# One scatter in place of two between attention and expert layers: residual rows carry their mean and reciprocal root, and sorted tiles are normalised behind their load

## What is computed

```python
x = x + attn(_layernorm(x), ...)          # linear attention: elu(q) (elu(k)^T silu(v)), head norm, gate, Wo
x = x + experts(_layernorm(x), itok, ctx) # 4 experts chosen by token number: silu(x G_e^T) * (x U_e^T), then D_e
x = x + ffn(_layernorm(x), W_up, W_gate, W_down)   # weights made ternary
```

## Time and profile before

| | us |
|---|---|
| median of 3 runs | 717.07 (715.48 to 717.67) |
| the profiled execution, its time | 716.13 |
| its span (first to last instruction) | 714.3 |
| TensorE busy | 686.1 |
| VectorE busy | 501.3 |
| ScalarE busy | 295.6 |
| GpSimd busy | 230.2 |

### The profile page before, as it was taken

The page is one execution under the profiler, slowest core; times in us unless marked ns, Lnnn a source line. Parts: engine busy times, 40 slices in busy tenths (PEclk is TensorE's granted clock), DMA queues, the critical chain, the costliest instruction groups (busy, mean ns, idle before and its releaser), DMA issues.

```text
span 714.3 us, 12503 instructions
## 1 busy us (share of the span) xinstructions
PE 686.1 (96%) x4776; PEld 453.1 (63%) x4776; DVE 501.3 (70%) x818; ACT 295.6 (41%) x450; POOL 230.2 (32%) x238
## 2 busy tenths in 40 slices
PE   6999999999999879999999999999999999999996
PEld 4556557557546465666554767777777777777772
DVE  5657846857756845656776778789877978677675
ACT  3466536635626324444332243434333434333331
POOL 4122803514325450000122053536453362425322
PEclk9999999999999999999999999999999999999999
DMA  8906006306406568671122020203120121101001
GB/s 223 384 20 225 6 14 223 118 0 235 118 1 226 188 220 318 245 261 34 45 53 53 1 53 1 53 1 67 46 39 15 27 85 27 27 1 60 1 1 59
DMA packets 57909, 67.36 MB, mean 94 GB/s; under 512 B 35072, under 2 KB 35072, under 8 KB 56832
## 3 DMA queue, kind: packets, MB, share of 16 engines
q1 hardware_dynamic: 54016, 54.03, 25.0%
q0 software_dynamic: 3840, 12.59, 4.8%
HBM read 46.69 MB, written 12.59 MB: 83 GB/s over the span
## 4 chain that ended last, share of the span: by engine, by line
PE 76%; DVE 8%; issue 4%; DMA 4%; ACT 3%; POOL 3%; SPq 1%; POOLq 0%; DVEq 0%; ACTq 0%
PE bank L1213 27%; PE bank L1492 25%; PE bank L1501 14%; PE bank L1206 4%; DVE region L820 2%; PE bank L1406 2%; PE bank L1370 2%; PE bank L1384 2%; DMA n<-sorted_tokens 2%; DVE late L816 1%; DMA sorted_residual<-rows,pos 1%; DMA stage<-in_L_attn_Wv_dram 1%; ACT stage L510 1%; POOL sorted_residual L343 1%; DVE region L824 1%
## 5 line engine op out<-in xcount | busy, mean ns | idle before, releaser
L1492 PE MATMUL bank<-w_att,region 128*128 128x256 f16 x1024 | 127.6, 273 | 0.0
L1501 PE MATMUL bank<-region,w_moe 128*128 128x512 bf16 x512 | 120.3, 379 | 2.2 <-POOL w_moe L440 1.4
L1492 PEld LDWEIGHTS bank<-w_att,region 128*128 128x128 bf16 x1024 | 100.1, 98 | 18.2 <-DVE tmpA L1138 0.2
L1213 PE MATMUL bank<-late,w_att 128*128 128x512 f16 x384 | 86.2, 379 | 3.6 <-DVE region L863 2.2
L1134 DVE TENSOR_TENSOR n<-bank,n 128x512 f32<-128x512 f32 x112 | 71.5, 685 | 19.7 <-PE bank L1492 17.7
L440 POOL TENSOR_TENSOR w_moe<-tmp,w_moe 128x512 f16<-128x512 f32 x30 | 36.5, 1215 | 142.9 <-ACT w_moe L660 142.9
L1501 PEld LDWEIGHTS bank<-region,w_moe 128*128 128x128 f16 x512 | 49.9, 98 | 50.5 <-POOL w_moe L440 1.7
L326 POOL TENSOR_SCALAR ve<-mv 128x1 f32<-128x1 f32 (+2 forms) x29 | 10.5, 362 | 198.1 <-DVE mv L700 197.9
L653 ACT ACTIVATE n<-n,qs 128x512 f32<-128x512 f32 x64 | 44.6, 719 | 65.3 <-DVE n L1134 65.3
L1213 PEld LDWEIGHTS bank<-late,w_att 128*128 128x128 f16 x384 | 37.0, 98 | 46.3 <-DVE region L863 3.0
L1492 PE MATMUL bank<-w_att,late 128*128 128x256 f16 x512 | 66.4, 273 | 0.0
(11 more groups left out here) (157 smaller groups left out, 1108.5 us busy)
## 6 DMA issues: line engine op xcount, KB each, us to landing
stage<-in_L_ffn_W_up_dram SPq DMA_DIRECT2D x8, 1024.0 KB
stage<-in_L_ffn_W_gate_dram SPq DMA_DIRECT2D x8, 1024.0 KB, 5.4
rows<-sorted_residual SPq DMA_DIRECT2D x4, 1026.0 KB, 9.6
stage<-in_ctx_dram SPq DMA_DIRECT2D x4, 1024.0 KB, 6.6
stage<-in_L_ffn_W_down_dram SPq DMA_DIRECT2D x4, 1024.0 KB
nrm<-in_L_ffn_W_down_dram SPq DMA_DIRECT2D x4, 1024.0 KB, 8.2
n<-sorted_tokens SPq DMA_DIRECT2D x16, 256.0 KB
rows<-in_x_dram SPq DMA_DIRECT2D x1, 3072.0 KB, 18.3
```

The lines of the kernel that those rows point to most:

```text
L1213: mm = pe.matmul(dst, lhs(*step), rhs(*step), start=(start and n == 0), stop=(stop and n == len(steps) - 1))
L1492: mm = pe.matmul(wk_ps[bank][:, q * H:(q + 1) * H], w[:, c + q, k * P:(k + 1) * P], x3S_part[slot][:, h, m, k], start=(h == 0 and k == 0), ...
L1501: mm = pe.matmul(ffy_ps[t][:, :], hid[:, u, h, q, (t % 2) * P:(t % 2 + 1) * P], tern[2][:, c + q], start=(begins and q == 0 and h == 0), s ...
```

## The change

Only one scatter is left. A row of `rows` and of `sorted_residual` gets two more columns, the row's mean and its reciprocal root (D + 3 = 515 numbers, 2060 bytes); `sorted_tokens` is gone. GpSimd writes both columns itself (`row_rsqrt`; in the last batch VectorE's aggregate writes straight into the row, and the power overwrites the variance). It scatters each residual tile behind that, without waiting for VectorE. SyncE loads each sorted tile with its two columns straight into `rows[:, i]`; the four loads of 1 MB and their semaphores are gone. VectorE then normalises tile i from `rows` into a slot of `n2` (`xs_norm`): tiles 0 and 1 ahead of step 0, tile i + 2 in step i between `xs_lo` and `y_add`. TensorE's transpose waits for that and no longer for the load. The four normalisations a batch are gone, and so is VectorE's wait for the scatters at a batch's end. The last batch's first sum stands between the two sign operations of the first unit.

```diff
-    xs_dram = nc.dram_tensor("sorted_tokens", (NT * P, D), F32, kind="Internal").ap()
-    x1_dram = nc.dram_tensor("sorted_residual", (NT * P, D + 1), F32, kind="Internal").ap()
+    x1_dram = nc.dram_tensor("sorted_residual", (NT * P, D + 3), F32, kind="Internal").ap()
...
         def sorted_tile(i):
-            sp.dma_start(xs_slot[i % 3], xs_v[:, i]).then_inc(s[f"xs_in{i % 3}"], 16)
-
-        def sorted_residual(b):
-            sp.dma_start(rows[:, T * b:T * b + T], x1_v[:, T * b:T * b + T]).then_inc(s[f"x1_in{b}"], 16)
+            sp.dma_start(rows[:, i], x1_v[:, i]).then_inc(s[f"xs_in{i % 3}"], 16)
...
-        sp.wait_ge(s["sign_b"], 1)
-        unit(1, 0)
-        sp.wait_ge(s["x1_sent"], 16 * NT)
-        sorted_residual(0)
...
-        for n in range(6):
+        for n in range(9):
+            sp.wait_ge(s["sign_b"], n + 1)
+            unit(1 + n // 3, n % 3)
             sp.wait_ge(s["tx_mm"], n + 1)
             sorted_tile(n + 3)
-            if n % 2 == 0:
-                sorted_residual(1 + n // 2)
-            sp.wait_ge(s["sign_b"], n + 4)
-            unit(2 + n // 3, n % 3)
...
+        def row_rsqrt(n, tiles, source, done, k):
+
+            mean, root = row_mean[:, n:n + tiles], row_root[:, n:n + tiles].rearrange("p n o -> p (n o)")
+            wait_apart(pool, "x2_aggr", n + tiles)
+            pool.tensor_scalar(ve[2][:, 0:tiles], source, LN_EPS, 0.0, ALU.add, ALU.add).then_inc(s[done], 1)
+            if tiles > 1:
+                pool.tensor_copy(mean, mv[2][:, :, 0:1]).then_inc(s[done], 1)
...
+            pool.tensor_tensor(root, ve[2][:, 0:tiles], halfs[:, 0:tiles], ALU.pow).then_inc(s[done], 1)
...
-        def scatter(b, t):
-
-            pool.wait_ge(s["x2_norm"], T * b + t + 1)
-            pool.indirect_dma_start(xs_dram, row_of(T * b + t), n2[:, t], None).then_inc(s["scattered"], 16)
-
-        def scatter_residual(b):
-            for n in range(T * b, T * b + T):
-                pool.indirect_dma_start(x1_dram, row_of(n), rows[:, n], None).then_inc(s["x1_sent"], 16)
+        def scatter(n):
+            pool.indirect_dma_start(x1_dram, row_of(n), rows[:, n], None).then_inc(s["scattered"], 16)
...
-                dve.wait_ge(s["rs2"], 2 * b)
-                for t in range(T):
-                    second_norm(b - 1, t)
...
-            if not first:
-                dve.wait_ge(s["scattered"], 16 * T * b)
...
+        def xs_norm(i):
+
+            dve.wait_ge(s[f"xs_in{i % 3}"], 16 * (i // 3 + 1))
+            if i >= 3:
+                dve.wait_ge(s["tx_mm"], i - 2)
+            dve.tensor_scalar(xs_slot[i % 3], x_tile(i), row_mean[:, i], row_root[:, i], ALU.subtract, ALU.mult).then_inc(
+                s["xs_norm"], 1)
...
             if i + 1 < NT:
                 xs_lo(i + 1)
+            if i + 2 < NT:
+                xs_norm(i + 2)
             if i > 0:
                 y_add(i - 1)
...
         def xs_transpose(i):
-            pe.wait_ge(s[f"xs_in{i % 3}"], 16 * (i // 3 + 1))
+            pe.wait_ge(s["xs_norm"], i + 1)
             pe.wait_ge(s["xs_lo"], i)
```

More of the change, by code:

```diff
@@ L120, in decoder @@
     row_id = rows[:, :, :].bitcast(I32)[:, :, D:D + 1]
+    row_mean, row_root = rows[:, :, D + 1:D + 2], rows[:, :, D + 2:D + 3]
     xT = late[:, 0].bitcast(F16).rearrange("p (i k s) -> p i k s", i=2, k=K)
@@ L169, in decoder @@
     names = """x_first0 x_first1 x_first2 x_first3 x_rest cols_in rows_in tok_in att_in0 att_in1 att_in2
-        att_in3 stage_in0 stage_in1 scattered x1_sent x1_in0 x1_in1 x1_in2 x1_in3 xs_in0 xs_in1 xs_in2 unit_in0 unit_in1 unit_in2
+        att_in3 stage_in0 stage_in1 scattered xs_in0 xs_in1 xs_in2 unit_in0 unit_in1 unit_in2
         out_done0 out_done1 out_done2 out_done3
@@ L258, in _ @@
             sorted_tile(i)
-        sp.wait_ge(s["sign_b"], 1)
-        unit(1, 0)
-        sp.wait_ge(s["x1_sent"], 16 * NT)
-        sorted_residual(0)
-        sp.wait_ge(s["sign_b"], 2)
-        unit(1, 1)
-        sp.wait_ge(s["sign_b"], 3)
-        unit(1, 2)
-        for n in range(6):
+        for n in range(9):
+            sp.wait_ge(s["sign_b"], n + 1)
+            unit(1 + n // 3, n % 3)
             sp.wait_ge(s["tx_mm"], n + 1)
             sorted_tile(n + 3)
-            if n % 2 == 0:
-                sorted_residual(1 + n // 2)
-            sp.wait_ge(s["sign_b"], n + 4)
-            unit(2 + n // 3, n % 3)
-        for i in range(9, NT):
+        for i in range(12, NT):
             sp.wait_ge(s["tx_mm"], i - 2)
@@ L355, in batch @@
                 for t in range(T):
-                    scatter(b - 1, t)
+                    scatter(T * b - T + t)
             if b < B - 1:
@@ L412, in _ @@
             rsqrt_tile(1, "o_aggr", T * (B - 1), t, "rs_o_last")
-        scatter_residual(B - 2)
-        rsqrt_tile(2, "x2_aggr", T * (B - 1), 0, "rs2_last")
-        for t in range(1, T):
-            rsqrt_tile(2, "x2_aggr", T * (B - 1), t, "rs2_last")
-            scatter(B - 1, t - 1)
-        scatter(B - 1, T - 1)
+        for t in range(T):
+            n = T * (B - 1) + t
+            row_rsqrt(n, 1, row_root[:, n], "rs2_last", t)
+            scatter(n)
         pool.memset(halfs[:, :], -0.5).then_inc(s["scatter_out"], 1)
-        scatter_residual(B - 1)
         def third_rsqrt(k):
@@ L847, in second_stats, with last_aggregate @@
             tile_stats(2, t, x_tile(T * b + t), "x2_stat")
-        def second_norm(b, t):
-            normalise(2, n2[:, t], x_tile(T * b + t), t, "x2_norm")
+        def last_aggregate(t):
+            n = T * (B - 1) + t
+            dve.wait_ge(s["x2_stat"], n + 1)
+            dve.bn_aggr(rows[:, n, D + 1:D + 3], st[2][:, t]).then_inc(s["x2_aggr"], 1)
         def ctx_lo(b, k):
@@ L970, in last_sum @@
             second_stats(B - 1, t)
-            aggregate(2, t, "x2_stat", T * (B - 1) + t + 1, "x2_aggr")
-        def last_norm(t):
-            dve.wait_ge(s["rs2_last"], 2 * t + 2)
-            second_norm(B - 1, t)
+            last_aggregate(t)
         dve.wait_ge(s["abs_done"], 3 * B)
@@ L998, in _ @@
         dve.wait_ge(s["scale_step"], 8)
-        signs_of(0, 0)
+        dve.wait_ge(s["unit_in0"], 16)
+        dve.wait_ge(s["u_mm"], NT)
+        positive(0, 0)
         last_sum(0)
-        last_sum(1)
-        last_norm(0)
-        last_sum(2)
-        last_norm(1)
-        last_sum(3)
-        last_norm(2)
-        last_norm(3)
+        negative(0, 0)
+        for t in range(1, T):
+            last_sum(t)
         dve.wait_ge(s["scatter_out"], 1)
         signs_of(0, 1)
+        def xs_norm(i):
[4 more added lines that the diff above has]
+                s["xs_norm"], 1)
         def xs_lo(i):
@@ L1021, in y_add @@
             dve.wait_ge(s["y_evac"], i)
-            if i < NT and i % T == 0:
-                dve.wait_ge(s[f"x1_in{i // T}"], 16)
             dve.scalar_tensor_tensor(out=x_tile(tile), in0=y_ps[:, :], scalar=own[:, i:i + 1], in1=x_tile(tile),
@@ L1101, in expert_step @@
                 weight_sum(1, 3)
+        xs_norm(0)
         xs_lo(0)
+        xs_norm(1)
         for i in range(STEPS):
```

16 lines of the change are left out of this document (10 added, 6 removed).

## The result

The changed kernel takes 712.49 us (median of 7 runs, 710.34 to 714.02), beside 716.96 us for the kernel before on the same chip (7 runs, 715.48 to 717.84). The ratio is 0.9936, with a 95% interval from 0.9917 to 0.9955: faster by 0.64%, or 4.5 us. The forecast was 2.3 us faster than before, 714.8 us, in a range from 712.5 to 716.9. The profiled execution took 713.10 us.

What follows compares the result with a forecast made beforehand. TensorE's own work was taken as the bound, 686.1 of 714.3 us. Gains of 1.1 us (start) and 1.2 (steps) sum to 2.3: 713.8 from the profiled execution, 714.8 against the runs' median, the forecast; range 712.5 to 716.9.

Steps and rivals of the forecast that it cites:

- GpSimd's chain: Hand-over: GpSimd's add, power and scatter take 2.37 us a tile; the last scatter ends 1.05 us sooner.
- Load issue to transpose ... about hides the new 0.64: Hand-over, tile 0: 0.59 us of slack in the 4.29 us link about covers the added normalisation and semaphore, 0.64 us.
- From transpose to first product: Hand-over, tile 0's transpose to the first expert product: no gain forecast, 0 us.
- So I add nothing: Scatter and load of 2060-byte rows: no added time, though a skill's rule gave 0.1 to 0.2 us.
- The end of the program: Behind the last output scatter, GpSimd's drain included: the prediction did not look there and counted no gain.
- Steps: Two long expert steps, 8.10 and 8.80 us, both become 7.85: 1.2 us gained, bounds 0 and 1.2.
- Rival 3: Expert steps: sign units issued earlier fill the DMA queue, only the start gains: 716.0 us; chance 0.08.
- Normalisations "cost nothing": Expert steps: VectorE's 16 normalisations of 0.54 us fit its idle time; cost nothing, without cover 7.6 us.
- Rival 2: Hand-over: the first expert product keeps the full clock, up to 1.43 us more gained, 713.4 us; chance 0.18.
- Rivals 1 and 4: Start hardly moves, 715.5 to 716.4 us, chance 0.18; normalisation waits for its tile, 728 us, 0.08 with other losses.
- Attention: Attention stage: TensorE waits for none of the removed work, so no gain or cost; without cover at most 5 us.

## Why the prediction was right or wrong

The direction was right, the size was not: 4.5 us and not 2.3, and 712.49 us lies just below the range.

- **GpSimd's chain**: right. The add under the sign operation took 1.09 us (forecast about 1.1), a tile's cycle is 2.31 (forecast 2.37), the last scatter came 1.17 us sooner (forecast 1.05). That the cycle came so close is luck in part: the scatter took 1.09 us and not 0.96, with 0.29 ahead of it and not 0.19, and behind it 0.03 and not 0.30. And what gave the 1.17 was less the earlier sum (0.33) than GpSimd's wait for the second tile's statistics, which the new order fills (about 0.84); the prediction does not name it.
- **"Load issue to transpose ... about hides the new 0.64"**: this is the step that failed. I took 3.7 us for a lone 256 KB load, from the start of the program, and saw only 0.59 us of slack in the 4.29 (forecast for the link: 4.34). Measured are 2.80 us from the issue to the start of the normalisation and 0.60 from there to the transpose, 3.40 in all: a gain of 0.89 where I had a loss of 0.05. The 4.29 us held the effect of four residual scatters in flight. They are among the things that the change removes, and I removed them from the steps' sum and not from the start's. With them held back in the kernel before, 0.92 of the 1.41 us marked "issue" in the earlier trace rows are gone. How those 0.92 divide between the landing and slower register loads is open; the landing alone took 0.70 us more with four spare scatters.
- **From transpose to first product** had no term. It gave 0.51 us by the two profiles, and what gave it stays open: it is not the scatters, since two kernels with scatters in flight took 2.16 us as well.
- **"So I add nothing"** for rows of 2060 bytes: wrong by 0.47 us in the landing of the last scatter. The 400 and 390 GB/s with many loads in flight did not show what a lone transfer's landing costs.
- **The end of the program** had no term. The drain gave 0.89 us, as much as the step that failed, and the prediction's sum held it at nothing without a reason.
- **Steps**: right, 1.20 us, both long steps are 7.85 us. Rival 3 (the jam stays) was false. Had only tile 3's load moved, it would have been nearly true: that kernel gained 0.25 of the 1.20 us.
- **Normalisations "cost nothing"**: right for 15 of 16; 0.15 us for the one under GpSimd's operation with two SBUF inputs. I had priced such a lock for the scale add and not looked for other places where it could occur.
- **Rival 2** (full clock in the first product): it happens in some executions of either kind: in one of the three profiles of kernels with the old hand-over, and in two of the nine with the new one that add no matmuls. It is chance in either and no part of the 4.0 us. Rivals 1 and 4 did not come: the start gained, and TensorE never waited for a normalisation after the first.
- **Attention** at nothing: right as far as can be told. Between 100 and 200 us TensorE's busy time is 99.05 us after and 99.06 before. From its first product of all to the first sign operation are 228.74 us before and 228.57, 228.53 and 228.47 after, while the two other kernels with the old attention stage have 228.22 and 229.22.

The terms by trace give 4.0 us, or 3.5 if the 0.51 us are chance. The medians give 4.5, with 3.2 to 6.0 by the interval of the ratio, so either can't be told from it.

## What to carry to other kernels

When a change takes transfers away, take them out of every wait that they overlap, not only of the one that names them: here a link that was taken as fixed shrank by 0.89 us, though a new operation had come into it. A transfer that lies alone on the critical path is priced by its landing, and here rows at uneven addresses landed 0.36 us or more later, which the throughput of many loads had not shown. An engine's order can cost as much as its work: look for what the engine waits for between two of its own instructions. Look past the last instruction that computes: what stands there may count things done long before.

## What the runs showed of the hardware that was not expected

- GpSimd's drain at the program's end grows with the indirect DMAs of the whole program, though the last batch of them is the same: 4.30 to 4.32 us with 32 (ten profiles), 4.47 with 36 (one), 5.19 to 5.20 with 48 (three).
- Four indirect scatters in flight slow a 256 KB load on another queue: 3.50 us until it is used and not 2.80 (2.69 to 3.26 over the profiles without them), and in the kernel before 4.29 us from load to transpose and not 3.36.
- Rows of 2048 bytes that start 12 bytes off took longer than rows of 2060 bytes at changing offsets: landing 2.73 against 2.13 to 2.51 us, load 4.07 against 2.69 to 3.26 us. That is one profile, of the slowest of five runs; the medians (0.9963 of the kernel before, against 0.9935 to 0.9939 for 2060-byte rows) go the same way.
- An indirect scatter that began 0.21 us before an operation of VectorE lasted until 0.12 us after that operation's end, 1.58 us in place of 1.09.
